# Deformable loop of a preactivation convolution net: transfers in eighths, sums from step 19 on, and edge products in the tile shape of the taps

## The reference, cut to what matters

```python
def dsc_axis(x, offset, weight, axis):
    off = jnp.transpose(offset, (0, 2, 3, 1))
    ...
    if axis == 'x':
        ix = wb + off
    ...
    s = grid_sample_zeros(x, ix, iy)
    return jnp.einsum('bchwk,ock->bohw', s, weight)
```

## Time and profile before

| | us |
|---|---|
| runs of before | 4863.48, 4871.4, 4862.8 (median 4863.48) |
| profiled execution, time | 4856.85 |
| profiled execution, span | 4855.0 |
| deformable stage in it | 1938.4 to 4358 |
| mean granted TensorE clock | 0.877 |

### The profile page before, as it was taken

How to read it: one execution, slowest core, us unless ns; L and a number is a source line. 1 busy time by engine, 2 the same in 40 slices (tenths; PEclk the granted TensorE clock), 3 DMA queues, 4 the chain that set the end, 5 groups by cost and what they waited for, 6 DMA issues and landing times. The chain is left out here.

```text
span 4855.0 us, 152250 instructions
## 1 busy us (share of the span) xinstructions
PE 3904.9 (80%) x63427; PEld 2346.6 (48%) x63427; DVE 2739.3 (56%) x4306; ACT 2207.0 (45%) x2870; POOL 1492.8 (31%) x1451
## 2 busy tenths in 40 slices
PE   7765558336999775699999999999999999980487
PEld 6665445222333321466666666566666656650132
DVE  4303646442333354478777787777777777774311
ACT  5500114231222243467666676666666666661111
POOL 0001200010000022446555455555555555540000
PEclk9955669657999987799999999999999999995799
DMA  3365669998777666331132321223212232209776
GB/s 97 71 122 146 181 133 255 269 293 200 221 215 213 185 257 194 68 68 40 43 78 56 71 64 32 63 51 71 65 40 54 55 70 62 49 26 314 184 164 160
DMA packets 790927, 606.61 MB, mean 125 GB/s; under 512 B 59272, under 2 KB 720392, under 8 KB 780844
## 3 DMA queue, kind: packets, MB, share of 16 engines
q1 hardware_dynamic: 638536, 442.77, 37.9%
q10 hardware_dynamic: 141840, 121.83, 8.3%
q0 software_dynamic: 9984, 33.56, 2.1%
HBM read 383.31 MB, written 214.70 MB: 123 GB/s over the span
## 5 line engine op out<-in xcount | busy, mean ns | idle before, releaser
L1495 ACT ACTIVATE df_t<-df_a 128x1024 f32<-128x1024 f32 x1024 | 1049.1, 1025 | 833.6 <-PE df_a L1580 833.6
L1442 POOL TENSOR_SCALAR df_t<-df_t 128x1024 f32<-128x1024 f32 x1024 | 1066.0, 1041 | 1069.1 <-ACT df_t L1495 1065.2
L1515 DVE TENSOR_SCALAR df_t<-df_d 128x1024 f32<-128x1024 f32 x1024 | 1252.1, 1223 | 223.9 <-PE df_d L1580 187.8
L1632 PE MATMUL df_o<-df_t,df_zs 128*32 128x128 f32 x36864 | 1257.6, 280 | 29.1 <-issue 24.4
L1632 PEld LDWEIGHTS df_o<-df_t,df_zs 128*32 128x32 f32 x36864 | 968.3, 111 | 348.9 <-DVE df_xo L1529 95.9
L1613 PE MATMUL df_z<-df_wz,df_x 32*128 32x288 f32 x4096 | 794.9, 464 | 8.5 <-issue 6.0
L1501 ACT ACTIVATE df_zs<-df_z 128x576 f32<-128x576 f32 x1024 | 660.6, 645 | 10.2 <-PE df_z L1613 10.2
L1580 PE MATMUL df_a<-df_ix,net_sel 7*128 7x512 bf16 (+1 forms) x2048 | 513.3, 390 | 4.1 <-DMA df_e<-edge 4.1
L1580 PE MATMUL df_d<-df_ix,net_sel 7*128 7x512 bf16 (+1 forms) x2048 | 409.9, 386 | 1.2 <-issue 1.2
L1521 DVE TENSOR_SCALAR df_t<-df_s 128x512 f32<-128x512 f32 x512 | 354.1, 692 | 57.1 <-PE df_s L1580 38.7
L1613 PEld LDWEIGHTS df_z<-df_wz,df_x 32*128 32x128 f32 x4096 | 313.8, 187 | 125.7 <-ACT df_zs L1501 115.7
(11 more groups left out here) (222 smaller groups left out, 4428.2 us busy)
## 6 DMA issues: line engine op xcount, KB each, us to landing
r_x<-x SPq DMA_DIRECT2D x64, 512.0 KB, 14.2
x<-r_x ACTq DMA_DIRECT2D x64, 512.0 KB, 11.8
gc_x<-x SPq DMA_DIRECT2D x240, 128.0 KB, 5.1
dc_x<-x SPq DMA_DIRECT2D x240, 128.0 KB, 3.2
dc_xt<-x_2t SPq DMA_DIRECT2D x240, 128.0 KB, 4.7
lc_x<-x SPq DMA_DIRECT2D x112, 256.0 KB, 5.2
fw_x<-in_x SPq DMA_DIRECT2D x32, 512.0 KB, 6.7
iv_x<-in_x SPq DMA_DIRECT2D x64, 256.0 KB, 4.8
```

Of the source, the lines that this page charges most:

```text
L1442: g.tensor_scalar(t, t, 1.0, 0.0, ALU.min, ALU.max).then_inc(clipped, 1)
L1495: act.activation(t, ps_a[:], ACT.Relu).then_inc(a_read, 1)
L1515: v.tensor_scalar(t, ps_d[:], 0.0, 1.0, ALU.max, ALU.min).then_inc(d_read, 1)
L1632: mm = pe.matmul(ps_o[32 * q:32 * q + 32, 0:P], Zs[:, n % 2, q, 32 * k:32 * k + 32], T[:, n % 2, slot(k), P * q:P * q + P], start=(start a ...
```

## The change

The change touches `deformable` and where the buffers of the earlier stages lie (they are now given back before this stage, which makes room; their work is the same). In `deformable`:

- The image, the plain sums, the columns and the rows are moved in eighths: one eighth after each step, at j = 2 to 9 (image and columns), 10 to 17 (rows) and 16 to 23 (plain sums). SyncE's list is written by step, and each step's part waits for the step before to be applied.
- `finish(b, c)` stands at step `late(c)` = 19, 20, 21, 22, 23, 26, 30, 34 of the half for c = 0 to 7, and `stats` and the store two steps later; `prepare` stands at j = 11 to 20.
- The edge product reads all 128 partitions with weights `Z0` that are zero outside each quarter's block (the same tile shape as `apply`), and stands behind the first `apply` of the step instead of ahead of the second. `Z0` is one buffer, loaded in quarters.
- `E` and `Z0` have to be zero outside their rows, so VectorE clears them, and it sets `IX` to one in GpSimd's stead (the line at GpSimd is gone); SyncE waits for all three before its first transfer. Its order at the start is: quarter 0 of the offsets, the image in 16 transfers, the store of the first column's products, quarters 1 to 3, then the first column's products back.

```diff
-        ZT, Z0 = s.sb("zt", [P, N9]), s.sb("z0", [P, 2, LINES * C])
+        ZT, Z0 = s.sb("zt", [P, N9]), s.sb("z0", [P, LINES * P])
...
+        def late(c):
+            return max(19 + c, 4 * c + 6)
...
-                def load_image(hh):
+                def load_image(hh, p):
                     b, a = divmod(hh, 2)
-                    if hh >= 2:
+                    if hh >= 2 and p == 0:
                         sp.wait_ge(z_full, 2 * LINES * (hh - 1))
-                    for q in range(4):
-                        sp.dma_start(X[a][32 * q:32 * q + 32].rearrange("c (j w) -> c j w", w=W), images[a][b, q]).then_inc(x_in[a], 16)
+                    for q in (2 * (p % 2), 2 * (p % 2) + 1):
+                        lines = slice(8 * (p // 2), 8 * (p // 2) + 8)
+                        sp.dma_start(X[a][32 * q:32 * q + 32].rearrange("c (j w) -> c j w", w=W)[:, lines], images[a][b, q][:, lines]).then_inc(x_in[a], 16)
                 def load_quarter(hh, c):
                     b, a = divmod(hh, 2)
-                    if hh:
-                        sp.wait_ge(applied, LINES * (hh - 1) + QL * (c + 1))
...
-                def move_first(hh):
-                    k = hh % 2
+                def store_first(hh):
                     sp.wait_ge(first_read, hh + 1)
-                    sp.dma_start(z0d[k], ZT[:]).then_inc(z0_out, 16)
+                    sp.dma_start(z0d[hh % 2], ZT[:]).then_inc(z0_out, 16)
+                def load_first(hh, c):
                     sp.wait_ge(z0_out, 16 * (hh + 1))
-                    if hh >= 2:
-                        sp.wait_ge(applied, LINES * (hh - 1))
                     for q in range(4):
-                        sp.dma_start(Z0[32 * q:32 * q + K9, k].rearrange("k (j o) -> k j o", o=C),
-                                     z0d[k, 32 * q:32 * q + 32].rearrange("j (k o) -> k j o", o=C)).then_inc(z0_in[k], 16)
+                        rows = Z0[32 * q:32 * q + K9].rearrange("k (j n) -> k j n", n=P)
+                        sp.dma_start(rows[:, QL * c:QL * (c + 1), 32 * q:32 * q + C],
+                                     z0d[hh % 2, 32 * q + QL * c:32 * q + QL * (c + 1)].rearrange("j (k o) -> k j o", o=C)).then_inc(z0_in[c], 16)
...
+                def load_plain(b, p):
+                    if p == 0 and b:
+                        sp.wait_ge(u_out, 128 * b)
+                        sp.wait_ge(counted, 8 * b)
+                    r = slice(PX // 32 * p, PX // 32 * (p + 1))
+                    sp.dma_start(U[:].rearrange("p j w -> p (j w)")[:, r], up[b][:, r]).then_inc(u_in, 16)
+                def store_columns(b, p):
+                    if p == 0:
+                        sp.wait_ge(kept, 8 * (b + 1))
+                    sp.dma_start(uy[b].rearrange("o h w -> h o w")[:, 4 * p:4 * p + 4],
+                                 YB[:, 4 * W * p:4 * W * (p + 1)].rearrange("p (o w) -> p o w", w=W)).then_inc(uy_out, 16)
+                def load_rows(b, p):
+                    if p == 0:
+                        sp.wait_ge(uy_out, 128 * (b + 1))
+                    q, lines = p // 2, slice(16 * (p % 2), 16 * (p % 2) + 16)
+                    sp.dma_start(YR[32 * q:32 * q + 32].rearrange("o (j w) -> o j w", w=W)[:, lines],
+                                 uy[b].rearrange("o (j q) w -> q o j w", q=4)[q][:, lines]).then_inc(uy_in, 16)
+                sp.wait_ge(ones, 3)
+                load_quarter(0, 0)
+                for p in range(8):
+                    load_image(0, p)
+                store_first(0)
+                for c in range(1, 4):
+                    load_quarter(0, c)
                 for c in range(4):
-                    load_quarter(0, c)
-                load_image(1)
-                move_first(0)
-                for hh in range(NH):
-                    b, a = divmod(hh, 2)
+                    load_first(0, c)
+                for n in range(ST):
+                    b, a, hh, j = place(n)
                     more = hh + 1 < NH
-                    if hh and more:
-                        load_image(hh + 1)
-                    if a == 0:
-                        if b:
-                            sp.wait_ge(u_out, 128 * b)
-                            sp.wait_ge(counted, 8 * b)
-                        sp.dma_start(U[:].rearrange("p j w -> p (j w)"), up[b]).then_inc(u_in, 16)
-                    else:
-                        sp.wait_ge(kept, 8 * (b + 1))
-                        for q in range(4):
-                            sp.dma_start(uy[b].rearrange("o h w -> h o w")[:, 8 * q:8 * q + 8],
-                                         YB[:, 8 * W * q:8 * W * (q + 1)].rearrange("p (o w) -> p o w", w=W)).then_inc(uy_out, 16)
-                        sp.wait_ge(uy_out, 64 * (b + 1))
-                        for q in range(4):
-                            sp.dma_start(YR[32 * q:32 * q + 32].rearrange("o (j w) -> o j w", w=W),
-                                         uy[b].rearrange("o (j q) w -> q o j w", q=4)[q]).then_inc(uy_in, 16)
-                    for c in range(4):
-                        if more:
-                            load_quarter(hh + 1, c)
-                        if more and c == 1:
-                            move_first(hh + 1)
-                        if a == 1:
-                            store_chunk(b, 2 * c)
-                            store_chunk(b, 2 * c + 1)
+                    if n:
+                        sp.wait_ge(applied, n)
+                    if more and 2 <= j < 10:
+                        load_image(hh + 1, j - 2)
+                    if a == 0 and 16 <= j < 24:
+                        load_plain(b, j - 16)
+                    if a == 1 and 2 <= j < 10:
+                        store_columns(b, j - 2)
+                    if a == 1 and 10 <= j < 18:
+                        load_rows(b, j - 10)
+                    if j % QL == 0 and n:
+                        c = j // QL - 1 if j else 3
+                        if (hh if j == 0 else hh + 1) < NH:
+                            load_quarter(hh if j == 0 else hh + 1, c)
+                    if j == 0 and n:
+                        load_first(hh, 3)
+                    if more and j == 23:
+                        store_first(hh + 1)
+                    if more and 26 <= j < 29:
+                        load_first(hh + 1, j - 26)
+                    for m in (n, n - LINES):
+                        if m >= 0 and place(m)[1] == 1:
+                            for c in range(8):
+                                if m - place(m)[3] + late(c) + 2 == n:
+                                    store_chunk(place(m)[0], c)
+                for c in range(8):
+                    if late(c) + 2 >= LINES:
+                        store_chunk(B - 1, c)
...
-                        if hh + 1 < NH and 10 <= j < 20:
-                            prepare(hh + 1, j - 10)
-                        m = n - 6
-                        if m >= 0 and place(m)[1] == 1 and m % 4 == 0:
-                            finish(place(m)[0], m % LINES // 4)
+                        if hh + 1 < NH and 11 <= j < 21:
+                            prepare(hh + 1, j - 11)
+                        for m in (n, n - LINES):
+                            if m >= 0 and place(m)[1] == 1:
+                                for c in range(8):
+                                    if m - place(m)[3] + late(c) == n:
+                                        finish(place(m)[0], c)
...
+                v.memset(IX[:], 1.0).then_inc(ones, 1)
+                v.memset(E[:], 0.0).then_inc(ones, 1)
+                v.memset(Z0[:], 0.0).then_inc(ones, 1)
...
-                        m = n - 9
-                        if m >= 0 and place(m)[1] == 1 and m % 4 == 0:
-                            stats(place(m)[0], m % LINES // 4)
-                for c in (6, 7):
-                    stats(B - 1, c)
+                        for m in (n, n - LINES):
+                            if m >= 0 and place(m)[1] == 1:
+                                for c in range(8):
+                                    if m - place(m)[3] + late(c) + 2 == n:
+                                        stats(place(m)[0], c)
+                for c in range(8):
+                    if late(c) + 2 >= LINES:
+                        stats(B - 1, c)
...
-                    if j == 0:
-                        pe.wait_ge(z0_in[hh % 2], 64 * (hh // 2 + 1))
+                    if j % QL == 0:
+                        pe.wait_ge(z0_in[j // QL], 64 * (hh + 1))
                     for q in range(4):
-                        pe.matmul(ps_o[32 * q:32 * q + 32, 0:P], Z0[32 * q:32 * q + K9, hh % 2, C * j:C * j + C],
-                                  E[32 * q:32 * q + K9, P * j:P * j + P], start=False, stop=False, tile_position=(32 * q, 32 * q))
+                        pe.matmul(ps_o[32 * q:32 * q + 32, 0:P], Z0[:, P * j + 32 * q:P * j + 32 * q + 32], E[:, P * j:P * j + P],
+                                  start=False, stop=False)
...
```

(5 more changed lines are left out.)

46 lines of the change are left out of this document (24 added, 22 removed).

## The result

The changed kernel takes **4662.98 us** (median of 4, 4659.5 to 4676.2) against 4863.14 (4840.5 to 4871.4): ratio 0.960, 95% interval 0.9563 to 0.9638, 200 us faster. The forecast was 123 us faster with a range down to 4710: the sign was right, the gain 77 us too small and the range missed it. The profiled execution is 4662.39 us, span 4660.3.

A forecast was written before the change was run, and what follows sets the result against it. TensorE was busy 2322.4 of the stage's 2419.6 us; plain step length and disturbances set the time. From 4856.85 profiled, -65 step, -73 disturbance, +15 start gave 4733.85, or 4740 against the median; range 4710 to 4788.

The forecast's parts named there:

- The step: Deformable loop: the edge products' new shape and place shorten a plain step from 4.32 us by 0.13, -65 us.
- Rival B: Plain step stays 4.32 us because later spreads make ScalarE's or VectorE's chain the bound; 4805 us, chance 0.08.
- The disturbance: Halves 1 to 15: of 93 us from GpSimd's row waits and TensorE's stands (idle without a releaser), 20 remain; -73 us.
- Rival A: TensorE's stands stay, instructions being late for another reason than backlog; only GpSimd's 32 us go; 4782 us, chance 0.13.
- 3 of the 4.2 us: Heaviest loop steps: transfers in eighths fill the engines about this long per step, then leave them free.
- GpSimd's sums: Finish from step 19: waiting for rows, 31.9 us, vanishes; clips delayed at steps 19 to 23 cost nothing.
- Rival C: Slower: transfers spread over 16 of 32 steps delay instruction packets and multiply the stands; 5020 us, chance 0.04.
- The start: Start of the deformable stage: VectorE's longer sets delay transfers, first edge product near 2003 against 1990.70; +15 us.
- +15 and -4: Up to the end of half 0: start +15 us and shorter steps -4 us, +11 together.

The follow-up runs named there:

- e3: Changed kernel with the edge products in their old shape and old place, all else new; 4735.9 us.
- e2: Changed kernel with the edge products in the new shape but at their old place, ahead of the second `apply`; 4673.6 us.
- e5: Changed kernel with the edge products in their old shape at the new place; 4727.6 us.
- e1: Kernel before with only the new layout: earlier stages' buffers given back ahead of the deformable stage; 4781.7 us.
- e4: Changed kernel with each group of eight transfer pieces issued in one step, as bursts, late sums kept; 4691.9 us.
- e10: Changed kernel with 32 bytes of padding ahead of the buffers of the deformable and later stages, earlier stages kept at 32 over 64; 4691.7 us.
- e6: Kernel before with 32 bytes of padding ahead of all stages behind the first layer; 4838.2 us.
- e12: Kernel before with 224 bytes of padding ahead of all stages behind the first layer, images at a multiple of 256; 4746.4 us.
- e14: Kernel before with the new layout plus padding that puts the buffers back at 32 over a multiple of 256; 4860.6 us.
- e13: Kernel before with 256 bytes of padding ahead of all stages behind the first layer, remainders modulo 256 unchanged; 4862.2 us.
- e8: Changed kernel with 32 bytes of padding that puts the stages ahead of the deformable one at a multiple of 64; 4668.7 us.
- e9: Changed kernel with another start: first image issued at once, GpSimd fills `IX` beside VectorE, first product's moves ahead of quarters 1 to 3; 4638.8 us.

## Why the prediction was wrong

**The step: right.** -65 was forecast for 512 steps; e3's loop is 64.0 longer in 480 of them. The plain step is 4.18, and the new wait on ScalarE's copy is there. One link was off: the second `apply` starts 1.98 us behind the first and not 2.15, and the wait for the copy, 0.19 and not 0.10, takes that back; z follows at 3.50 (3.48 in the forecast), which sets the step. The products' move buys at most 2 us of loop (e2, e5), the shape does the rest. Rival B, a step that stays at 4.32, is out.

**The disturbance: right mechanism, mis-sized.** I took 20 of 93 us as left; nothing was (loop of e3 91.5 shorter than before, edge products alike). That bulk transfers keep TensorE's instructions away stands up: in the loop before, each of the 24 stands ended 2 to 4 us behind a packet of the instruction queue, and in 21 of them this packet came after a gap of over 7 us without one, where only one gap in ten is that long. The largest gap is 13.4 us before and 8.0 after. Rival A, that the stands stay, is out. What I had wrong is the size of a backlog. I read 86.6% as nearly full, 174 GB/s. The shares of packets overlap, and the same queue shows more in the kernel before, here from 2732.4 to 2745.2:

```profile
q1 hardware_dynamic: 5366, 2.71, 118.5%
```

These 2.71 MB are 212 GB/s, so 174 was no ceiling, and "3 of the 4.2 us" rested on it. And I did not see how much hung on the buffers' remainder. With the old bursts it alone takes 21 us of stands and 79 us of low clock off the loop (e1). With aligned buffers, the bursts bring back only 7 stands of 13.6 us (e4). In eighths the remainder does not matter (e10). Two cures for one loss: 53 by the layout alone, 91 with both, and 91 by the eighths and the late sums without the layout. In that order, 53 is the layout, 16 the eighths (e4), and the 22 that remain, an estimate, lie with the late sums, since GpSimd waits 38.5 us for rows in e1 and for none in e4. Bursts with late sums at remainder 32 were not run, so there the two stay unsplit. The mean packet, 45.9 ns before, takes 40.2 in e1, 30.5 in e10 and 28.8 with both, in the ratio of 54.1% to 86.6%.

**GpSimd's sums: right.** GpSimd waits for no rows, and behind the start TensorE waits for GpSimd nowhere in the stage: at steps 19 to 23 the clips come in time. Rival C, stands that multiply with the spread transfers, is out as well: two stands are left, both in half 0.

**The start: too high.** +15 and -4 became -3.6. VectorE's three sets end at 1960.5, not 1963.0, since it sets an element in 0.84 ns and not the 1 ns that I read off sets of 128 elements, which carry a fixed part (128 elements at 0.84 ns are 107 of their 165). The first products were in SBUF 14.2 us behind the image's issue (1965.2 to 1979.4) and not 17.5. The faster landing is in part the layout's too: e10, with its images at remainder 32, takes 16.2. The three quarters and the return took 17.6 us, as forecast (17.8). With the 2.5 us of the sets that makes 6 us to the first edge product. From there to the end of half 0 it is 136.5 us, before 146.5: 10 less, 3 by the shape (e3 has 139.8). The other 7 go with the clock, 20 us of it low there before and 4 after, and no stand lies there in either. That the change brought them is not shown: e1, e6, e12 and e14, with the old shape and the old bursts, have 140 us and 4 to 6 us of low clock, e13 has 146.5 and 20. I had put all of half 0's excess to the start.

**The steps that failed: no term for the layout, and 18 us too little for the disturbance.** The text ahead of the prediction says that the buffers of the earlier stages are given back and that their work is the same, and the prediction gave that no line, and put nothing for what lies behind the loop. The layout moved all buffers of the deformable stage and of the stages behind it to another remainder modulo 256, and 35.6 us behind the loop are 46% of the miss. e10 takes 32 us of tail back with 32 bytes. The tail of one execution varies: with remainder 0 it was 470 to 491 us in twelve profiled kernels of either code, with remainder 32 it was 502 to 509 in four, so the shift is worth some 26 us and the rest of the 35.6 is chance of the profiled pair (e6, at 64, has 485). In medians on one chip e10 is 23 us slower than e8.

**The account of the 77 us**: behind the loop 36; disturbance 73 against 91, 18; start and half 0, 14; step 3; together 71. The tail's term alone would not have saved the range: less 36, it would have begun at 4674; less the 18 of the disturbance too, at 4656. The last 6 are that I started from a profiled execution 6.6 us below its median, and the one of after is at its median.

Not settled: why a shift of 32 bytes costs a packet under load so much more than its extra beats, and why TensorE's stands cost the clock for so long in some halves; why the tail at remainder 64 was short in e6 though its transfers landed late.

## What to carry to other kernels

- A change in what is allocated moves every buffer behind it. Compare the addresses modulo 256 of all buffers that transfers write, before and after; look at the landing times of transfers that the diff does not touch. Padding of 224 bytes made the kernel before 107 us faster.
- Two cures for one loss do not add: measure each with the other in place. Spread transfers hid the alignment in the loop, but not in the last convolution and the graph convolution, where transfers are waited for.
- A rate read off small instructions overprices a large one; take one of the same order of size or keep both as bounds.

## What the hardware showed

- A 128 KB transfer of 512-byte rows into SBUF landed in 3.5 us with rows at a multiple of 256 bytes, 4.6 at 64 over, 5.1 at 32 over (e12, e6, before). A multiple of 64 is not enough (e6, e8).
- VectorE sets 16384 bf16 in 13.71 us and 4096 f32 in 3.47: 0.84 and 0.85 ns an element. GpSimd sets the same 16384 in 13.75 us, alone (before) and beside VectorE (e9). By the Trainium skill, VectorE: DVE Perf Modes, section Zero memsets can be issued as uint32 (trn2), a memset takes one cycle per element, an estimated 1.04 ns at the page's 0.96 GHz; the trace has it a fifth faster.
- The last convolution, with the same instructions, had the higher granted clock where its transfers landed faster (0.98 and 4.6 us against 0.92 and 5.2): of its 28 us, 14.5 are TensorE's busy time and the rest waiting. That the waits brought the clock down is read from the two going together, and was not tested by itself; in e6 the clock was 0.99 with landings of 5.1.
